# Expert weights split early and parked in DRAM, gather, stores and output rearranged, in a one-core attention and mixture-of-experts kernel

## What is computed

```python
x = x + attn(cond(x, itok))          # gated FFN, shared and by type, then 16-head causal attention
x = x + ffn(cond2(x, itok))          # three shared and two chosen FFNs mixed, then top-2 of 8 experts

def ffn(x):                          # E = 8 experts, capacity 10 tokens per batch and expert
    h = relu(x @ rW1 + rb1); h = relu(h @ rW2 + rb2)             # the router
    scales = softmax(h @ rW3 + rb3); top2 = top_k(scales, 2)
    dispatched[e, b, pos] = x                                    # gather, 10 slots each
    eout = relu(dispatched @ eW1[e] + eb1[e]) @ eW2[e] + eb2[e]
    return sum(topk_scales * eout[e, b, pos])                    # combine
```

## Time and profile before

| | |
|---|---|
| runs shown | 2497.40, 2498.56, 2502.49 us; median 2498.56 us |
| profiled execution | 2495.63 us |
| its span, first to last instruction | 2494.0 us |
| PE busy | 2346.7 us (94%) |
| DVE, ACT, POOL busy | 1173.9, 1076.1, 250.2 us |
| matmuls of the router, L908 and L919 | 86.3 and 336.7 us |
| matmuls of the experts, L1027 and L1039 | 125.8 and 126.7 us |
| mean granted TensorE clock | 0.973 of full |

### The profile page before, as it was taken

One profiled execution on the slowest core, in us unless ns is written; L12 is line 12 of the kernel. 1 busy time (PEld: TensorE's weight loads), 2 busy tenths in 40 slices (PEclk: granted clock), 3 DMA queues, 4 the chain that ended last, 5 costly groups with the idle time before them and its releaser, 6 DMA issues.

```text
span 2494.0 us, 51324 instructions
## 1 busy us (share of the span) xinstructions
PE 2346.7 (94%) x18894; PEld 1544.2 (62%) x18895; DVE 1173.9 (47%) x2337; ACT 1076.1 (43%) x2061; POOL 250.2 (10%) x399
## 2 busy tenths in 40 slices
PE   6999999996999899999999999997999999989994
PEld 2444688885888444444446888886444444467774
DVE  5553455445998442332323433334344445265543
ACT  3553455443666442332323333332444444466660
POOL 0000000003432000000000000000000000025553
PEclk9999999998999899999999999998999999999995
DMA  3330011002333230120110100001111110012242
GB/s 119 102 101 34 31 52 51 34 18 65 91 100 74 82 127 25 60 76 26 43 42 22 47 13 13 13 13 60 51 35 34 50 34 17 0 60 91 92 123 79
DMA packets 145911, 136.93 MB, mean 55 GB/s; under 512 B 80992, under 2 KB 129632, under 8 KB 139360
## 3 DMA queue, kind: packets, MB, share of 16 engines
q1 hardware_dynamic: 126720, 76.94, 10.5%
q0 software_dynamic: 16016, 55.60, 6.5%
q10 hardware_dynamic: 3024, 2.36, 0.3%
HBM read 90.80 MB, written 34.60 MB: 50 GB/s over the span
## 4 chain that ended last, share of the span: by engine, by line
PE 82%; SPq 5%; ACT 4%; DVE 3%; issue 3%; DMA 2%; POOL 0%; DVEq 0%; POOLq 0%; ACTq 0%
PE ps L664 31%; PE ps L681 24%; PE ps L919 13%; PE ps L908 3%; PE ps L1039 3%; PE ps L1027 3%; SPq L373 2%; ACT misc L1187 1%; DMA arena<-in_x 1%; SPq L480 1%; SPq L479 1%; PE ps L746 1%; ACT arena L1186 1%; PE ps L778 1%; PE ps L933 1%
## 5 line engine op out<-in xcount | busy, mean ns | idle before, releaser
L664 PE MATMUL ps<-xh,arena 128*128 (+1 forms) x5376 | 908.6, 312 | 18.3 <-DVE xh L1433 10.3
L681 PE MATMUL ps<-misc,arena 128*128 128x256 f16 (+1 forms) x4128 | 727.5, 313 | 9.3 <-DVE misc L1503 5.7
L664 PEld LDWEIGHTS ps<-xh,arena 128*128 (+1 forms) x5376 | 527.4, 98 | 290.4 <-issue 27.7
L681 PEld LDWEIGHTS ps<-misc,arena 128*128 (+1 forms) x4128 | 402.8, 98 | 224.1 <-issue 9.1
L1507 DVE SCALAR_TENSOR_TENSOR misc<-ps,misc 128x256 f16<-128x256 f32 (+1 forms) x480 | 254.9, 531 | 544.8 <-ACT misc L1119 544.0
L1119 ACT ACTIVATE misc<-ps 128x256 f16<-128x256 f32 (+1 forms) x480 | 225.0, 469 | 555.1 <-PE ps L664 555.1
L919 PE MATMUL ps<-arena 128*128 128x512 f16 x1536 | 336.7, 379 | 0.0
L919 PEld LDWEIGHTS ps<-arena 128*128 128x128 f16 x1536 | 148.2, 98 | 173.4
L1770 DVE TENSOR_TENSOR arena<-misc,arena 128x512 f16<-128x512 f32 x128 | 88.6, 692 | 230.3 <-ACT arena L1254 230.3
L1501 DVE TENSOR_TENSOR arena<-ps,misc 128x256 f32<-128x256 f32 (+1 forms) x208 | 105.1, 506 | 144.3 <-ACT misc L1115 143.5
L1115 ACT ACTIVATE misc<-ps 128x256 f32<-128x256 f32 (+1 forms) x208 | 93.5, 449 | 162.7 <-PE ps L664 162.5
(11 more groups left out here) (238 smaller groups left out, 2056.2 us busy)
## 6 DMA issues: line engine op xcount, KB each, us to landing
wstage<-in_m_w POOLq DMA_DIRECT2D x16, 1024.0 KB, 5.3
arena<-src_d SPq DMA_DIRECT2D x64, 256.0 KB, 3.7
src_d<-misc SPq DMA_DIRECT2D x24, 512.0 KB, 3.1
wstage<-in_c_wi POOLq DMA_DIRECT2D x6, 1024.0 KB, 5.3
wstage<-in_r_w POOLq DMA_DIRECT2D x5, 1024.0 KB, 5.6
cexp_d<-misc SPq DMA_DIRECT2D x18, 256.0 KB, 2.5
src_d<-misc SPq DMA_DIRECT2D x18, 256.0 KB, 2.5
cshare_d<-misc SPq DMA_DIRECT2D x8, 512.0 KB, 3.1
```

Of the source, the lines that this page charges most:

```text
L664: last = mm(ps[:, bank, col:col + p.n], weight(off, half, g, wp, k * F + f * 128), xh[:, xp, k, ds(start, p.n)], start=(k == 0 and n == 0) ...
L681: last = mm(ps[:, 4 + 2 * half + m, 0:p.n], weight(place[0], half, 2 if p.gated else 1, wp, f * D + m * 128), hid[:, st % 4, hp, 0:p.n], s ...
```

## The change

Seven edits come together:

- The 14 matrices of experts 1 to 7 are split during the router, in quarters of 512 columns: ACT `piece_high` and DVE `piece_low` at stages 9 to 15 of each chunk, 7 x 8 = 56 pieces, into a small buffer `piece` of two; POOL stores each piece to `parts_d` in DRAM. During the experts SP loads the finished halves, two transfers of 1 MB for each expert, into place. ACT's and DVE's splitting between the experts' stages is gone.
- The gather's tokens are laid out by slot, then batch. Its 32 units cover four token tiles, one of the two 128-row halves of x and one f16 half each; ACT evacuates the even units and DVE the odd ones, 640 columns at a time, where both evacuated 320 columns of each of 32 tiles.
- With that order a tile of expert outputs is two slots of 64 batches, and `expert_store` needs 2 transfers for each queue and tile (10 for each queue and expert, where there were 30), each of 32 rows.
- `x1_d` is laid out by batch, so x1_store becomes two transfers of 256-byte pieces.
- `yo` holds all 64 batches, DVE L1850 becomes one instruction of 256 columns for each pair, and no store is waited for before the end.
- PE runs 40 matmuls (`keep_clock`) before attention.
- ACT's loop over the router's chunks is written out.

```diff
@@ weights
-            wait = (s["l_mm"], 8) if e == 1 else (s["m_out"], 2 * (e - 1))
-            loads += [(a["m_w1"][e], MOE_W[e % 2][0], SW, wait), (a["m_w2"][e], MOE_W[e % 2][1], SW, wait)]
+            loads += [(a["m_w1"][e], None, SW, None), (a["m_w2"][e], None, SW, None)]
@@ ACT, router
+            def piece_high(n):
+                i, q = FIRST_MOE + n // 4, n % 4
+                if q == 0:
+                    act.wait_ge(s[f"w_in{i % 2}"], 16 * (i // 2 + 1))
+                if n >= 2:
+                    act.wait_ge(s[f"mw_st{n % 2}"], 16 * (n // 2))
+                fn(piece[:, n % 2, 0, :], wstage[:, i % 2, q * 512:(q + 1) * 512], ACT.Copy, scale=SW).then_inc(s["w_hi"], 1)
...
+                    if st >= 9:
+                        piece_high(c * 7 + st - 9)
-            with act.Fori(1, 7) as c:
-                router(c, False, True)
-            router(7, False, False)
+            for c in range(1, 8):
+                router(c, False, c < 7)
@@ DVE, router
+            def piece_low(n):
+                i, q = FIRST_MOE + n // 4, n % 4
+                dve.wait_ge(s["w_hi"], 4 * i + q + 1)
+                last = v.scalar_tensor_tensor(piece[:, n % 2, 1, :], wstage[:, i % 2, q * 512:(q + 1) * 512], SW, piece[:, n % 2, 0, :],
+                                              ALU.mult, ALU.subtract)
...
+                    if st >= 9:
+                        piece_low(c * 7 + st - 9)
@@ POOL
+            for n in range(8 * (NE - 1)):
+                pool.wait_ge(s["mw_lo"], n + 1)
+                pool.dma_start(parts_d[n // 4, :, :, (n % 4) * 512:(n % 4 + 1) * 512], piece[:, n % 2]
+                               ).then_inc(s[f"mw_st{n % 2}"], 16)
+                if n % 4 == 3 and FIRST_MOE + 2 + n // 4 < len(loads):
+                    fetch(FIRST_MOE + 2 + n // 4)
@@ SP, experts
+            def expert_weights(e):
+                if e >= 2:
+                    sp.wait_ge(s["m_out"], 2 * (e - 1))
+                for w in range(2):
+                    slot = MOE_W[e % 2][w]
+                    sp.dma_start(arena[:, slot * SLOT:(slot + 1) * SLOT], parts_d[2 * (e - 1) + w].rearrange("p h n -> p (h n)")
+                                 ).then_inc(s[f"mw_in{e % 2}"], 16)
...
             for e in range(NE):
                 for t in range(5):
+                    if t == 3 and e + 2 < NE:
+                        expert_weights(e + 2)
                     sp.wait_ge(s["eo_lo"], e * 5 + (t + 1))
                     expert_store(sp, "eo_st", e, t, 0)
@@ SP, attention
-                sp.dma_start(x1_d[:, :, ds(c * CH, CH)], x1).then_inc(s["x1_out"], 16)
+                for k in range(KC):
+                    sp.dma_start(x1_d[:, c * GB:(c + 1) * GB, k, :], x1[:, k, :].rearrange("p (b n) -> p b n", b=GB)
+                                 ).then_inc(s["x1_out"], 16)
@@ stores of expert outputs
+            slot = e * CAP + 2 * t + h
+            for j in range(2):
+                lo = h * 64 + j * 32
+                queue.dma_start(ebf[j][slot:slot + 1, :, :], eo[lo:lo + 32, t % 4, :, :].rearrange("p h n -> p (h n)")
+                                ).then_inc(s[f"{stored}{t % 4}"], 16)
@@ output
+            places = range(first, B, 3)
...
-                    dve.wait_ge(s[f"fin_st{u // 2}"], q * 16 * FIN_ST[u // 2])
-                    dve.wait_ge(s[f"fin_sp{u // 2}"], q * 16 * FIN_SP[u // 2])
...
+                v.scalar_tensor_tensor(yo[:, t].rearrange("p b k n -> p (b k n)"), ps[:, u, 0:256], 1 / (SEO * SCW),
+                                       x1f[q][:, 2 * u:2 * u + 2].rearrange("p b k n -> p (b k n)"), ALU.mult, ALU.add
@@ PE
+            def keep_clock(bank, count):
+                for _ in range(count):
+                    mm(ps[:, bank, :], identb[:, :], causal[:, :, :].rearrange("p h n -> p (h n)"), start=True, stop=True)
...
             gate(4, 2, 1, ce)
+            keep_clock(3, 40)
@@ PE, gather (ACT does units 0, 2, ..., DVE units 1, 3, ...)
+                (g, k), part = divmod(unit // 2, KC), unit % 2
+                if unit >= 3:
+                    pe.wait_ge(s["xe_lo" if unit % 2 == 0 else "xe_hi"], (unit - 3) // 2 + 1)
+                for j in range(4):
+                    t = g * 4 + j
+                    last = mm(ps[:, 2 * (unit % 3) + j // 2, (j % 2) * 2 * SLOTS:(j % 2 + 1) * 2 * SLOTS],
+                              xh[:, part, k, t * 128:(t + 1) * 128], d01[:, t].rearrange("p b s -> p (b s)"),
```

More of the change, by code:

```diff
@@ L70 @@
 XE_SLOT, CT_SLOT = 5, 11
+UNITS = 8 * KC * 2
 EBF_SLOT = 1
@@ L1291, in _, with gather @@
             router(0, True, True)
-            with act.Fori(1, 7) as c:
-                router(c, False, True)
-            router(7, False, False)
-            def gather(t):
-                act.wait_ge(s["dp_mm"], t + 1)
-                fn(xe_pair(0, t), dp(0, t), ACT.Copy).then_inc(s["xe_hi"], 1)
+            for c in range(1, 8):
+                router(c, False, c < 7)
+            def gather(unit):
+                act.wait_ge(s["dp_mm"], unit + 1)
+                fn(xe_group(0, unit), dp(unit), ACT.Copy).then_inc(s["xe_hi"], 1)
             soft(7)
-            for t in range(NP):
-                gather(t)
-                if t == 7:
+            for unit in range(0, UNITS, 2):
+                gather(unit)
+                if unit == 10:
                     one_hots(7)
-                if t == 10:
+                if unit == 12:
                     turned_weights(7)
@@ L1783, in _, with gather @@
                 router(c)
-            def gather(t):
-                dve.wait_ge(s["dp_mm"], t + 1)
-                v.tensor_copy(xe_pair(1, t), dp(1, t)).then_inc(s["xe_lo"], 1)
+            def gather(unit):
+                dve.wait_ge(s["dp_mm"], unit + 1)
+                v.tensor_copy(xe_group(1, unit), dp(unit)).then_inc(s["xe_lo"], 1)
             logits(7)
-            for t in range(NP):
-                if t == 4:
+            for unit in range(1, UNITS, 2):
+                if unit == 5:
                     choose(7)
-                if t == 8:
+                if unit == 9:
                     place(7)
-                gather(t)
+                gather(unit)
             def bias_scaled():
```

167 lines of the change are left out of this document (64 added, 103 removed).

## The result

The changed kernel takes 2503.85 us in the median (2496.11 to 2506.47, 20 runs) against 2498.27 (2493.18 to 2502.83, 20 runs) for the one before: ratio 1.0019, 95% interval 1.0013 to 1.0026. Forecast were 2484 us. The profiled execution has a span of 2500.8 us, 6.8 more than before. (One execution of a later kernel, the old order with x1 as before, took 7529.95 us and is left out of its ratio.)

The account below looks back on a forecast made before the run. PE bounds router and experts, the chain over SP's x1 store and x loads bounds attention. +9.2 + 0 + 0 - 0.5 - 8.5 - 15.0 = -14.8 us from 2498.56 gives 2483.8, say 2484 us; own range 2477 to 2492.

Parts of the forecast that it names:

- Attention, +9.2: Attention: SP's second x1 store delays x by 0.65 us in 15 turns, less 0.5: 9.2 us lost.
- The rival on small writes: Attention: 256-byte writes behind x1_store hold up x on the transfer engines; 2511 us at four times the mean; chance 0.10.
- `keep_clock`, 0: Ahead of attention: 40 matmuls start the projection 2.5 us later but speed it up; 0, bounds 3 lost, 1 won.
- Gather, -0.5: Gather: DVE's 16 evacuations of 640 columns take 12.8 us, against 13.5 for 32 of 320; 0.5 us gained.
- Experts, -8.5: Experts: ACT's waits caused by SP's 30 stores per expert go; 3.24 + 5.30 = 8.5 us gained, bounds 5 and 10.
- the wait ahead of the combination, -9.1: End: SP issues four transfers for the last two tiles, so PE combines sooner; 9.1 us gained.
- landing adds 1.6 to 2 us: End: after the last stores are issued by 2443.9, landing takes 1.6 to 2 us, so PE combines at 2445.8.
- the buffer is wanted only some 13 us later: Experts: 2 MB loads stand ahead of two tiles' stores in SP's queue, but ACT needs the buffer only 13 us later.
- 5 us, if they delay a store after all: Experts: lower bound of the 8.5 us gain, should the new 2 MB loads delay a store.
- Combination and output, -5.9: End: beyond the 9.1 us wait, the last vector result is 6.9 us earlier, less 1 us for the output's transfers.
- What is late next is the output's transfers: End: output transfers finish between 2470 and 2472, where PE's end and one landing give 2470; 1 us taken off.
- the four rivals: Small writes delay x (0.10); second issue hidden in attention (0.09); router pieces stall PE (0.08); gather reads at half rate (0.06).

Follow-up runs that it names:

- the old order with x1 as before: Changed kernel with gather, row order and expert-output stores as in the kernel before, and x1 stored as before too: 2485.10 us, ratio 0.9939.
- the rows spread: Changed kernel with only the place of the experts' outputs altered, the 32 rows of one store going to 32 different partitions: 2479.88 us.

## Why the forecast was wrong

It said 2484 us and the chip says 2503.85, 20 us more. By its own steps:

- **Attention, +9.2.** Right in its mechanism, too large in its size: +8.7 in the two profiles first taken, but 6.6 between the means of all. The chain goes over SP's stores as it was said:

```profile
743.00 0.91 ACT L1238 ACTIVATE arena<-arena,bias 128x256 f32<-128x256 f32 x2 [1.69 <-DMA arena<-in_x]
```
```profile
748.60 0.70 DVE xh L1694
749.32 0.39 SPq L550
749.75 0.51 SPq L550
```

  SP issues the two stores in 0.94 us from the first start to the last end, where the one of before took 0.59: 0.35 us more, not 0.65. ACT's idle time is 1.69 us where the earlier trace rows has 1.32. By the means a turn grew by 6.6 / 15 = 0.44 us. The rival on small writes fell: the stores of 256-byte pieces land in 2.2 us in the median, against 2.5 for those of 1 KB pieces before. The Trainium skill ("DMA: Bandwidth & Descriptors", Specifications) has a read-modify-write below 512 B; these rows show no cost of it.
- **`keep_clock`, 0.** Right in its mechanism. PE's 40 matmuls bring the clock up and the projection takes 2.78 us in place of 4.74:

```profile
571.03 9.93 PE L752 MATMUL ps<-causal,identb 128*128 128x512 bf16 x40
580.99 2.78 PE L763 MATMUL ps<-arena 128*128 128x256 f16 x24
590.27 0.61 PE L776 MATMUL ps<-causal,identb 128*128 128x512 bf16 x1 [6.50 <-DMA arena<-arena]
```

  From the gate's first matmul to the first scores, the 13 profiles with it take 23.1 to 25.3 us (mean 24.2) and the four without it 25.0 to 28.2 (mean 26.0). Both pairs of kernels that differ by it alone are faster with it, by 2.9 and 1.5 us. That points to a gain of 1 to 3 us, where the forecast had 0 and at most 1, but the intervals overlap in both pairs.
- **Router, 0.** Right, by the row of its stage above. PE L936, the router's big group, has no idle time ahead of it:

```profile
L936 PE MATMUL ps<-arena 128*128 128x512 f16 x1536 | 336.7, 379 | 0.0
```

- **Gather, -0.5.** Off by 1.6 to 2 us: router and gather together take 463.0 to 464.0 us in the eleven profiles with the new gather and 462.0 to 462.8 in the six with the old one, 1.1 between the means and 1.6 between the two profiles first taken. The price of an instruction was near, also with the stride:

```profile
2209.23 6.87 DVE L1820 CAST arena<-ps 128x640 f16<-128x640 f32 x8 [0.32 <-PE ps L1019]
```

  That is 0.86 us each against 0.80 to 0.82, and at half rate it would be 1.6. What makes the rest of the difference I didn't try.
- **Experts, -8.5, and the wait ahead of the combination, -9.1.** Here it failed, and it is one step: "landing adds 1.6 to 2 us" at the end, and in the experts that the queue is empty long before. I counted a store by its issue, and took its landing from stores that put 12 or 13 rows into a partition and went over ten partitions for each tile. The new order of rows puts a tile's 128 KB into two partitions. That lands in 10 us instead of 2, and the tiles come in groups, 2 us behind one another, so the stores pile up. At the end that alone is the miss. In the experts it takes the weights as well: the step "the buffer is wanted only some 13 us later" had room for 2 MB of loads and a landing of 2 us, not for a landing of 10 behind them; without the loads the experts take 167.04 us in spite of the slow stores. With the rows spread the two terms measured -8.5 and -10.2. So the size of the gain was right for the number of stores, and wrong for the place they write to. The bound I had set ("5 us, if they delay a store after all") didn't hold the loss of 5.7, since it kept the landing at 2 us.
- The reading of the earlier trace rows behind that step was right, and more so than I used it: "taking the splitting away gives PE nothing more", and the loss is SP's issue. With the old order and the weights split early the experts stay at 175.16; with the stores divided otherwise in the kernel before they take 166.99.
- **Combination and output, -5.9.** Right up to the last vector result: -7.1 where -6.9 was forecast. PE's 384 matmuls run in 20.64 us without a gap, at the lower clock in every 4 us that I read, of which one is:

```profile
2476.00:2480.00 4.00, 4.00 (x79) 4.00 (x77) 2.64 (x7) 0.00 (x0) 2.37 (x5) 0.50 0.73 209
```

  PE is wholly busy and stays at 0.50, 1.2 GHz, as in the earlier trace rows. Where the Trainium skill ("TensorE: Matmul & The Clock Gate", Part 1) lets the clock rise after sustained work, this stretch of 20 us of 80-row matmuls does not show it; the measurement decides, and keeping 54 ns each was right. The last step, "What is late next is the output's transfers", for which 1 us was taken off, is not what the traces show. In both kernels the transfers have landed some 8 us before the span ends, and POOL's closing instruction ends it. It takes 10.03 and 10.28 us, so the two cancel and the term cost nothing: luck, as the kernels where it takes 4.6 to 8.9 us show.

None of the four rivals is what happened: those that lose time looked for it in attention, the router and the gather. That a store could land later was looked at only for the weights ahead of it, not for its own destination.

## What to carry to other kernels

Fewer and larger transfers save issue time, but count where the bytes go: a store's landing time from the trace holds only for stores with the same spread over partitions. When a layout is turned around, ask for each transfer how many partitions it touches and how many KB arrive at one of them before its reader. And when uneven turns have a wait with nothing on an engine to release it, price the queue that issues (here 0.76 us on SP for a store of 13 rows, 0.50 on POOL) and try the division between queues first; it was a small edit, and in the kernel before it was worth 12.6 us. Last, look at what stands at the very end of the span: a closing instruction that differs by up to 5.6 us between kernels can hide or fake the effect of a change elsewhere.

## What the runs showed of the hardware

- Stores into two neighbouring partitions at once are slow and share a rate. 128 KB took 10 us (13 KB/us); half of it, by either way of halving, 5 to 8 us, counted the same way, from SP's first issue to the last landing. Spread over 32 partitions the same bytes were in place 2.7 us after the first issue (4.1 in one expert). While it lasts, the transfer engines are held: over the experts they are 0.60 busy at 91 GB/s, and 0.28 busy at 93 GB/s with the rows spread. Weights of 1 MB take 10.8 us to land in place of 6.3.
- This rate isn't fixed. In stores of 8 rows the same 128 KB of a first tile were in place after 7 to 9 us, 2 to 4 us behind the last issue, with both queues writing; stores of 16 rows took as long as those of 32. Why 8 rows pass and 16 don't stays open. It is no way out here, since SP starts one only every 0.68 us.
- Stores of whole rows into one partition cost POOL 0.48 to 0.50 us to issue whatever their size (32, 16, 13 or 8 rows), and 0.60 where a store goes to two partitions. On SP they cost 0.50 to 0.59 us for 32 rows, 0.76 for 13 rows and 0.64 for 8.
- POOL's closing DRAIN ends the span in all 17 profiles; it takes 4.6 to 10.3 us. It repeats within 0.01 us among kernels with the same number and form of stores (10.27 or 10.28 in six, 5.70 in three, 6.43 or 6.44 in three), and doesn't simply follow their number: with 210 transfers issued by POOL it takes 10.3 us in those six and 4.6 in the one whose stores go to two partitions.
